# A graph layer with a feed-forward on one core: sums of gathered messages made, copied, turned and added in pairs

## What is computed

```python
hx = jnp.einsum('ni,rio->rno', layernorm(x), weight)           # 6250 nodes, 256 features, 8 relations
agg = jax.ops.segment_sum(hx[edge_type, src], dst, num_segments=6250)   # 206250 edges, sorted by dst
x1 = x + agg * 0.5 ** 0.5 + h_bias + (layernorm(x) @ loop_weight) * 0.5 ** 0.5
xn = layernorm(x1)
w = xn @ wr + br                                               # one weight a node
y = (gelu(xn @ w1 + b1) @ w2 + b2) * w                         # 256 -> 1024 -> 256
out = x1 + xn + where(node is among the 3124 largest w, y, 0)
```

## Time and profile before

| | us |
|---|---|
| median of 3 runs | 2587.57 (2576.79 to 2591.49) |
| profiled execution, its own time | 2560.34 |
| span of that execution | 2558.7 |
| PE busy | 1869.3 (73%) |
| PE weight loads | 1529.2 (60%) |
| POOL busy | 1548.9 (61%) |
| DVE busy | 776.9 (30%) |
| ACT busy | 697.8 (27%) |

### The profile page before, as it was taken

One profiled execution on the slowest core, in us unless ns is written; L12 is line 12 of the kernel. 1 busy time (PEld: TensorE's weight loads), 2 busy tenths in 40 slices (PEclk: granted clock), 3 DMA queues, 4 the chain that ended last, 5 costly groups with the idle time before them and its releaser, 6 DMA issues.

```text
span 2558.7 us, 25060 instructions
## 1 busy us (share of the span) xinstructions
PE 1869.3 (73%) x8680; PEld 1529.2 (60%) x8680; DVE 776.9 (30%) x1714; ACT 697.8 (27%) x1341; POOL 1548.9 (61%) x1737
## 2 busy tenths in 40 slices
PE   1237878777877877887877877877877877877881
PEld 0126657666665665665666666756656665666671
DVE  6112322232232232232232232232232232222337
ACT  5102223223222222222322322223223223223240
POOL 2666666666666666666666666666666666666500
PEclk9568888887887898887988988888988887887895
DMA  7533333333333333333333333333333333333315
GB/s 254 158 88 98 98 99 95 93 103 97 97 103 95 97 101 97 96 100 97 99 103 97 97 105 97 98 102 99 97 103 98 98 103 97 95 101 96 85 33 179
DMA packets 126598, 265.50 MB, mean 104 GB/s; under 512 B 30091, under 2 KB 73003, under 8 KB 126473
## 3 DMA queue, kind: packets, MB, share of 16 engines
q0 software_dynamic: 79168, 218.05, 29.6%
q1 hardware_dynamic: 47304, 45.83, 5.7%
HBM read 244.52 MB, written 19.25 MB: 103 GB/s over the span
## 4 chain that ended last, share of the span: by engine, by line
PE 55%; another core or an unknown queue 21%; issue 10%; ACT 8%; DVE 3%; DMA 1%; SPq 1%; DVEq 0%; POOL 0%; ACTq 0%; POOLq 0%
PE bank L642 21%; PE bank L670 13%; PE bank L688 7%; PE bank L696 7%; PE bank L652 4%; ACT hidden L541 2%; ACT stage L506 2%; PE bank L672 2%; ACT L541 1%; DMA acc<-in_edge_type 1%; DVE acc L1060 1%; ACT L528 1%; DMA w_sb<-in_L_ffn_w 1%; ACT normed_t L533 1%
## 5 line engine op out<-in xcount | busy, mean ns | idle before, releaser
L404 POOL DMA_INDIRECT messages<-normed_table,gather_rows x1614 | 1531.0, 949 | 854.3 <-issue 433.3
L642 PE MATMUL bank<-messages,onehot 128*128 128x256 f32 x3228 | 929.3, 423 | 124.9 <-issue 100.6
L642 PEld LDWEIGHTS bank<-messages,onehot 128*128 128x128 f32 x3228 | 642.6, 213 | 248.9 <-issue 179.0
L919 DVE SCALAR_TENSOR_TENSOR sums<-bank,regular,sums 128x256 f32 x538 | 259.9, 483 | 1657.4 <-remote 850.8
L506 ACT ACTIVATE stage<-bank 128x256 f32<-128x256 f32 x538 | 207.3, 388 | 1737.4 <-remote 1013.9
L652 PE MATMUL bank<-ident,stage 128*128 128x128 f32 x1076 | 234.4, 297 | 254.8 <-issue 158.8
L670 PE MATMUL bank<-rel_sb,closed 128*128 128x256 f32 x1568 | 361.6, 384 | 8.7 <-ACT closed L512 8.7
L652 PEld LDWEIGHTS bank<-ident,stage 128*128 128x128 f32 x1076 | 151.5, 152 | 336.1 <-issue 283.1
L688 PE MATMUL bank<-normed_t,w_sb 128*128 128x128 f32 x1568 | 240.0, 316 | 131.2 <-ACT normed_t L533 72.2
L670 PEld LDWEIGHTS bank<-rel_sb,closed 128*128 128x128 f32 x1568 | 302.3, 193 | 53.3 <-ACT closed L512 10.8
L688 PEld LDWEIGHTS bank<-normed_t,w_sb 128*128 128x128 f32 x1568 | 225.4, 229 | 147.1 <-ACT normed_t L533 85.6
(11 more groups left out here) (136 smaller groups left out, 519.8 us busy)
## 6 DMA issues: line engine op xcount, KB each, us to landing
messages<-normed_table,gather_rows POOLq DMA_INDIRECT x1614
normed_x<-normed_table SPq DMA_DIRECT2D x49, 128.0 KB
residual<-resid SPq DMA_DIRECT2D x49, 128.0 KB
x_block<-in_x SPq DMA_DIRECT2D x48, 128.0 KB
node_out<-acc SPq DMA_DIRECT2D x12, 512.0 KB
messages<-in_x POOLq DMA_DIRECT2D x6, 896.0 KB, 14.9
normed_table<-messages SPq DMA_DIRECT2D x6, 896.0 KB, 8.0
messages<-residual SPq DMA_DIRECT2D x6, 896.0 KB, 10.1
```

The lines of the kernel that those rows point to most:

```text
L404: pool.indirect_dma_start(messages[0:EP, g % RING, j * D:(j + 1) * D], None, table, bass.IndirectOffsetOnAxis(ap=gather_rows[0:EP, g, j:j ...
L642: last = nc.tensor.matmul(banks[g % STAGES][:, 0:D], onehot[0:EP, g % SLOTS, j, :], messages[0:EP, slot, j * D:(j + 1) * D], start=(j == 0 ...
L919: V.scalar_tensor_tensor(sums[:, :, to], banks[TURNS[g % 2]][:, 0:D].rearrange("p (n m) -> p n m", m=W), regular[:, 0:1], sums[:, :, to], ...
```

## The change

The tick stays, but sums, copies, turns and additions come at odd ticks, for two groups at once. The two groups of a pair share a bank of PSUM: the first in columns 0 to 255, the second in 256 to 511. One copy of 512 columns takes both to `stage`, four transposes turn them, and two additions add them. The turn is of the pair two before the one that is summed at that tick (LAG 4 in place of 2), and the closing tick of a block is made odd. `summed`, `staged` and `turned` count pairs; POOL waits once a pair, at its even group. The block's later steps move to later ticks: up from 9 to 10, gelu from 10 to 12, down from 12 to 14, `ffn_leave` from 13 to 16.

In the head, a partition holds seven neighbouring rows of the features (runs of 7 KB in memory in place of 1 KB). The sources are loaded first on SyncE's queue; destinations and types follow the features on POOL's. `index_stage` comes behind the last chunk in place of behind the third.

In the tail, the last block's up product is made in halves ahead of the first two counts, its down product in quarters ahead of the last four, and its `ffn_leave` comes behind the eighth round. The selection waits for the last w alone.

```diff
-    LAG = 2
+    LAG = 4
...
-    TURN, TURN_TAKE, UP, GELU, DOWN, LEAVE = 7, 8, 9, 10, 12, 13
+    TURN, TURN_TAKE, UP, GELU, DOWN, LEAVE = 7, 8, 10, 12, 14, 16
...
-    closing = {g + LAG: b for b, g in enumerate(closes)}
+    closing = {(g | 1) + LAG: b for b, g in enumerate(closes)}
...
-        table_chunks = table.rearrange("(c v p) d -> c p v d", p=P, v=CH)
+        table_chunks = table.rearrange("(c p v) d -> c p v d", p=P, v=CH)
...
-        stage = sb("stage", [P, STAGES, D])
+        stage = sb("stage", [P, STAGES, 2 * D])
...
-            sp.wait_ge(pads_set, 3)
-            for a, to in ((dst, dst_s), (src, src_s), (edge_type, type_s)):
-                sp.dma_start(to[:, 0:full_tiles, :], a[0:full_tiles * P * GE].rearrange("(t p e) -> p t e", p=P, e=GE)).then_inc(edges_in, 16)
-                sp.dma_start(to[0:rest, full_tiles, :], a[full_tiles * P * GE:NG_FULL * GE].rearrange("(p e) -> p e", e=GE)).then_inc(edges_in, 16)
-                sp.dma_start(to[rest:rest + 1, full_tiles, 0:E - NG_FULL * GE],
-                             a[NG_FULL * GE:E].rearrange("(p e) -> p e", p=1)).then_inc(edges_in, 16)
+            sp.wait_ge(pads_set, 1)
+            sp.dma_start(src_s[:, 0:full_tiles, :], src[0:full_tiles * P * GE].rearrange("(t p e) -> p t e", p=P, e=GE)).then_inc(src_in, 16)
+            sp.dma_start(src_s[0:rest, full_tiles, :], src[full_tiles * P * GE:NG_FULL * GE].rearrange("(p e) -> p e", e=GE)).then_inc(src_in, 16)
...
-            sp.wait_ge(summed, NG)
+            sp.wait_ge(summed, NG // 2)
...
+            pool.wait_ge(pads_set, 1)
...
+            x_chunks = x[0:last_first * P, :].rearrange("(c p v) d -> c p v d", p=P, v=CH)
...
+            nc.gpsimd.memset(dst_s[:, GT - 1, :], -1).then_inc(pads_set, 1)
+            nc.gpsimd.memset(type_s[:, GT - 1, :], 0).then_inc(pads_set, 1)
+            pool.wait_ge(pads_set, 3)
+            for a, to in ((dst, dst_s), (edge_type, type_s)):
+                pool.dma_start(to[:, 0:full_tiles, :], a[0:full_tiles * P * GE].rearrange("(t p e) -> p t e", p=P, e=GE)).then_inc(edges_in, 16)
+                pool.dma_start(to[0:rest, full_tiles, :], a[full_tiles * P * GE:NG_FULL * GE].rearrange("(p e) -> p e", e=GE)).then_inc(edges_in, 16)
+                pool.dma_start(to[rest:rest + 1, full_tiles, 0:E - NG_FULL * GE],
+                               a[NG_FULL * GE:E].rearrange("(p e) -> p e", p=1)).then_inc(edges_in, 16)
             nc.gpsimd.memset(ident[:, :], 0.0).then_inc(node_pad_set, 1)
...
-                if g >= RING:
-                    pool.wait_ge(summed, g - RING + 1)
+                if g >= RING and g % 2 == 0:
+                    pool.wait_ge(summed, (g - RING) // 2 + 1)
...
-            def stage_group(g):
-
-                act.wait_ge(summed, g + 1)
-                nc.scalar.activation(stage[:, g % STAGES, :], banks[g % STAGES][:, 0:D], ACT.Copy).then_inc(staged, 1)
+            def stage_pair(q):
+
+                act.wait_ge(summed, q + 1)
+                nc.scalar.activation(stage[:, q % STAGES, :], banks[q % STAGES][:, :], ACT.Copy).then_inc(staged, 1)
...
-                if g < NG:
-                    stage_group(g)
+                if g < NG and g % 2 == 1:
+                    stage_pair(g // 2)
...
-            def sum_group(g):
-
-                slot = g % RING
-                if g % 2 == 0:
-                    pe.wait_ge(onehot_ready, g // 2 + 1)
-                pe.wait_ge(gathered[slot], 16 * J * (g // RING + 1))
-                for j in range(J):
-                    last = nc.tensor.matmul(banks[g % STAGES][:, 0:D], onehot[0:EP, g % SLOTS, j, :],
-                                            messages[0:EP, slot, j * D:(j + 1) * D], start=(j == 0), stop=(j == J - 1))
+            def sum_pair(q):
+
+                pe.wait_ge(onehot_ready, q + 1)
+                for g in (2 * q, 2 * q + 1):
+                    slot = g % RING
+                    pe.wait_ge(gathered[slot], 16 * J * (g // RING + 1))
+                    for j in range(J):
+                        last = nc.tensor.matmul(banks[q % STAGES][:, g % 2 * D:(g % 2 + 1) * D], onehot[0:EP, g % SLOTS, j, :],
+                                                messages[0:EP, slot, j * D:(j + 1) * D], start=(j == 0), stop=(j == J - 1))
                 last.then_inc(summed, 1)
 
-            def turn_group(g):
-
-                if g >= 2:
-                    pe.wait_ge(sum_taken, g - 1)
-                pe.wait_ge(staged, g + 1)
-                for k in range(KC):
-                    last = nc.tensor.transpose(banks[TURNS[g % 2]][:, k * P:(k + 1) * P],
-                                               stage[:, g % STAGES, k * P:(k + 1) * P], ident[:, :])
+            def turn_pair(q):
+
+                if q >= 2:
+                    pe.wait_ge(sum_taken, 2 * q - 2)
+                pe.wait_ge(staged, q + 1)
+                for k in range(2 * KC):
+                    last = nc.tensor.transpose(banks[TURNS[q % 2]][:, k * P:(k + 1) * P],
+                                               stage[:, q % STAGES, k * P:(k + 1) * P], ident[:, :])
                 last.then_inc(turned, 1)
 
...
-            def ffn_first(b):
-                pe.wait_ge(ffn_norm_t, b + 2)
-                pe.wait_ge(ffn_done, 2 * b + 1)
-                for m in range(HC):
+            def ffn_first(b, first=0, past=HC):
+                if first == 0:
+                    pe.wait_ge(ffn_norm_t, b + 2)
+                    pe.wait_ge(ffn_done, 2 * b + 1)
+                for m in range(first, past):
                     for k in range(KC):
                         last = nc.tensor.matmul(banks[5 + m // 4][:, m % 4 * P:(m % 4 + 1) * P],
                                                 w1_sb[:, k, m * P:(m + 1) * P], normed_t[:, k, :],
                                                 start=(k == 0), stop=(k == KC - 1))
-                last.then_inc(ffn_up, 1)
-
-            def ffn_second(b):
-                pe.wait_ge(ffn_gelu, b + 2)
-                for m in range(HC):
+                if past == HC:
+                    last.then_inc(ffn_up, 1)
+
+            def ffn_second(b, first=0, past=HC):
+                if first == 0:
+                    pe.wait_ge(ffn_gelu, b + 2)
+                for m in range(first, past):
                     last = nc.tensor.matmul(banks[5][:, 0:D], hidden[:, m, :], w2_sb[:, m, :],
                                             start=(m == 0), stop=(m == HC - 1))
-                last.then_inc(ffn_down, 1)
+                if past == HC:
+                    last.then_inc(ffn_down, 1)
 
             pe.wait_ge(rel_in, 16 * KC)
             pe.wait_ge(ffn_w_in, 32)
             pe.wait_ge(loop_in, 16)
...
-                if LAG <= g < NG + LAG:
-                    turn_group(g - LAG)
-                if g < NG:
-                    sum_group(g)
+                if LAG <= g < NG + LAG and g % 2 == 1:
+                    turn_pair((g - LAG) // 2)
+                if g < NG and g % 2 == 1:
+                    sum_pair(g // 2)
...
-                if g - UP in closing:
+                if closing.get(g - UP, NB - 1) < NB - 1:
                     ffn_first(closing[g - UP])
-                if g - DOWN in closing:
+                if closing.get(g - DOWN, NB - 1) < NB - 1:
                     ffn_second(closing[g - DOWN])
 
             for r in range(8):
+                if r < 2:
+                    ffn_first(NB - 1, r * HC // 2, (r + 1) * HC // 2)
+                elif r >= 4:
+                    ffn_second(NB - 1, (r - 4) * HC // 4, (r - 3) * HC // 4)
                 pe.wait_ge(counts_in, r + 1)
                 nc.tensor.matmul(banks[0][:, 0:15], one_rows, pick_counts[:, :], start=True, stop=True).then_inc(counts_out, 1)
             pe.wait_ge(counts_in, 9)
...
-                if c == 2:
-                    index_stage()
+            index_stage()
...
-                dve.wait_ge(turned, g + 1)
+                if g % 2 == 0:
+                    dve.wait_ge(turned, g // 2 + 1)
                 to = bass.ds(places[g % LOAD], W)
                 if g:
                     dve.wait_ge(sum_taken, g)
-                if g - 1 in closed_at:
-                    dve.wait_ge(carried, closed_at[g - 1] + 1)
+                for before_it in (g - 1, g - 2):
+                    if g % 2 == 0 and before_it in closed_at:
+                        dve.wait_ge(carried, closed_at[before_it] + 1)
                 if g - 1 - WAIT_CLEAR in closed_at:
                     dve.wait_ge(slot_cleared, closed_at[g - 1 - WAIT_CLEAR] + 2)
-                V.scalar_tensor_tensor(sums[:, :, to], banks[TURNS[g % 2]][:, 0:D].rearrange("p (n m) -> p n m", m=W),
+                V.scalar_tensor_tensor(sums[:, :, to], banks[TURNS[g // 2 % 2]][:, g % 2 * D:(g % 2 + 1) * D].rearrange("p (n m) -> p n m", m=W),
                                        regular[:, 0:1], sums[:, :, to], ALU.mult, ALU.add).then_inc(sum_taken, 1)
 
             def carry(b):
...
```

(17 more changed lines are left out.)

27 lines of the change are left out of this document (15 added, 12 removed).

## The result

| | us |
|---|---|
| before, median of 4 runs | 2586.26 (2576.79 to 2591.49) |
| after, median of 4 runs | 2703.93 (2701.44 to 2705.57) |
| ratio after to before, 95% interval | 1.0458 (1.0427 to 1.0490) |
| profiled execution after: own time, span | 2701.44, 2699.7 |

What follows compares the result with a forecast made beforehand. The prediction took POOL's gathers and their ring waits for late-seen TensorE sums as the bound. From 2560.3, head -9, end -9.5, drain +1 and middle 0 gave 2542.8; with 27.2 for the median, 2570 us, range 2430 to 2655.

Steps and rivals of the forecast that it cites:

- Head, -9: Before the first gather: index work moved behind the last feature chunk lets gathers start earlier; -9 us, bounds 0 and -14.
- End, -9.5: After the last gather: selection no longer waits for the last feed-forward, whose halves and quarters are mostly hidden; -9.5 us.
- my mark of 1 us: Tail check in the changed profile: the selection should start within 1 us of the last weights.
- Drain, +1: Behind the last sum: 2 more transposes and a longer copy, about +1 us.
- Turns: TensorE's waits ahead of transposes, 158.8 + 80.8 us, would thin out; taken as worth nothing, middle being POOL's.
- Pairs at the relation products: Both products between two pair sums, 11.0 us against 7.5 of gathers; cost between 0 and 108 us, taken as 0.
- The bound of +108: Upper bound in the middle for longer ring gaps at the relation products: (5.3 - 3.1) x 49 = 108 us.
- The lateness: TensorE's finished work seen late (8.1 us) during gather runs, soon after POOL stops; copies should still start many microseconds late.
- The 27 us between profile and median: Median of before lies 27.2 us above its profiled execution; the same was expected of the changed kernel.
- the sum of 2542.8: Forecast of the changed kernel's profiled execution: 2560.3 - 9 - 9.5 + 1 + 0 us.
- The second: Rival: coarser ring release lengthens the gap at the relation products, 2624 to 2678 us; chance 0.27.
- The first: Rival: freed TensorE waits shorten the ring's gaps, 40 us or more in the middle; chance 0.20.

Runs made afterwards that it cites:

- paced_later_again: products_later with a 64-column memset on GpSimd and a wait for its end before each group of gathers; 2693.7 us against 2558.0 before, chip B.
- head_tail: Kernel before with the changed head and end only, single groups, old turn lag and ticks; 2560.5 us against 2587.6 before, chip A.
- products_later: Changed kernel with relation products and following steps two ticks later, two spare ticks before the last block; 2549.0 us on A, 2558.5 on B when repeated.
- close_ahead: Changed kernel with ScalarE's closed copy ahead of the closing tick's pair copy, two spare ticks before the last block; 2611.6 us against 2587.6 before, chip A.
- after_third: The changed kernel, unedited, on prompt-signal chip E; 2185.6 us against 2195.1 before, ratio 0.9958.
- release_by_group: Changed kernel with each group freeing its ring place at its own sum's end, copies, turns and adds still paired; 2674.1 us against 2587.6 before, chip A.
- one_behind_later: products_later with LAG = 2, the turn one pair behind the sum; 2173.5 us against 2195.3 before, chip C.
- both_ahead: close_ahead with ScalarE's copy of the turned loop input ahead of the pair copy too; 2174.2 us against 2195.1 before, chip D.

## Why the prediction was wrong

*Head, -9.* Right in kind, a low figure: -14.0 measured, the bound I had set. The trace of after puts the wait before the first gather down to ScalarE's copy of the keys, but the gathers ask only for the store of the features and for the tables of rows, which were taken long before the keys. In paced_later_again the same wait is put down to the store, as I had it:

```profile
55.02 0.16 POOL L415 MEMSET pace<- 128x64 f32 x1 [26.17 <-DMA normed_table<-closed]
```

*End, -9.5.* Right on its own: -12.3 in head_tail. In the changed kernel it is spoiled. The selection starts at 2639.39, 6.6 us behind the last weight (2632.58 + 0.21), and my mark of 1 us fails, because it stands behind `ffn_leave` of the last block but one:

```profile
2632.58 0.21 DVE L980 TENSOR_SCALAR w_all<-w_block,br_b 128x1 f32<-128x1 f32 x1
2633.26 5.29 PE L709 MATMUL bank<-w_sb,hidden 128*128 128x256 f32 x16 [4.43 <-ACT hidden L551]
2638.66 0.42 DVE L986 TENSOR_TENSOR acc<-bank,b_b 128x256 f32<-128x256 f32 x1 [5.86 <-PE bank L709]
2639.39 0.18 DVE L1030 TENSOR_SCALAR routing<-w_all 128x49 int32<-128x49 int32 x1
```

*Drain, +1.* Mis-sized: +22.6 against head_tail behind the last gather, of which 6.6 are this later start of the selection. From the last gather to the last weight after takes 84.1 us (2548.73 to 2632.79) and head_tail 67.6 (2431.64 to 2499.19). I had counted two transposes and a copy. But the drain begins with a wait of 9.16 us for `closed`, where head_tail's first one behind the last gather is 2.25 us, and its later hand-overs stand tighter too (4.17 us at the next `closed`, 4.43 at the down product):

```profile
2557.43 5.65 PE L680 MATMUL bank<-rel_sb,closed 128*128 128x256 f32 x16 [9.16 <-ACT closed L522]
```

*Turns.* Their waits fell from 240 to 78 us, and the kernel got no faster by it, as I had said. The reason is not the one I gave: the waits turned up elsewhere, as the next item says.

*Pairs at the relation products, "I take 0 here as well, since a longer gap also lets the late signals through".* This is the step that failed. It is the larger part of the 117 us that the pairs cost between the gathers, where I had put nothing. The rows of before gave the spacing of TensorE's work: 11.0 us of work against 7.5 us of ring. I asked how long the products keep the sums away, and never whether the products' own inputs would be there. TensorE's queue holds several instructions that need a late result: a turn needs the copy of a sum two back, the products need, by way of `closed`, the copy of the sum one back. In the kernel before, the turns came up first and took the waits: 240 us, and 8.7 us in 4 at the products. In the changed one a turn asks for what is two pairs old and passes, and TensorE runs on until the first instruction that asks for what is one pair old. The waits fell by 162 us at the turns (240 to 78) and rose by 151 at the products (8.7 to 159.4), but they didn't just change places: at the up product they rose as well, from 130.7 to 243.1, and I can't say how much of that comes of the same hand-overs. I had taken the first as a gain of nothing, and left out the others. What makes the same wait dearer there is only argued: behind a turn comes a sum, which frees the ring; behind the products' wait come 8 us of products, and in the block shown GpSimd used up its ring over them. That the place of the products and what they ask of ScalarE make most of the loss, three comparisons show: products_later gives back 155 us, and 123 on B, where only the tick of the products parts it from the slowest kernel; close_ahead, which but for its two spare ticks only gets `closed` ready earlier, gives back 92. The bound of +108 left out the same thing; it lies just under the 117.

*The lateness.* The mark held (7.2 us where 8.1 had been). But I wrote of it as something that comes with gathers. after_third has the same row of gathers without any, so gathers alone don't bring it; the sort of chip has a part, which the trace of one chip couldn't tell. I also wrote that finished work is seen soon after GpSimd has had to stop: 47 of the 120 late copies of after start with gathers going on.

*The 27 us between profile and median.* I carried them over to the changed kernel. Its profiled execution is 2701.4 with a median of 2703.9; head_tail's is 2561.7 with 2560.5. The offset belonged to one execution of the kernel before. By own times the sum of 2542.8 missed by 158.6: middle +144.7, of which 27.8 are this offset and 116.9 the pairs, end and drain +18.8, head -5.0. As a base for the median the 27 us were in place (2587.6 - 17.5 = 2570); as an offset between profile and median that every kernel has they were not.

*Rivals.* The second (coarser release, 2624 to 2678, chance 0.27) named the right place, the right sign and a size that was too small, for another reason than the right one: release_by_group shows that the coarser release itself is 30 us of it. The first, freed waits, didn't occur.

A page and this trace: ScalarE's table load ahead of `closed` takes 1.28 us, with 1.31 between its neighbours (1273.14 + 0.38 to 1274.83). The Trainium skill, page "ScalarE: Activation LUTs", section "What ACT_TABLE_LOAD costs", gives 1283 ns for the load, which agrees, and some 1.4 us of drain more, which this place doesn't show; 94 of the 97 loads of after have the same 1.31 us between their neighbours. By the page's sum, as an estimate, the products would have waited 1.4 us longer than they did.

On the lateness itself, "Perfetto Trace Analysis" of the Trainium skill, section "Summary: the profiler window per engine type", says that a TensorE row ends at an estimated time and leaves out the way of the signal. The 7.2 us may thus lie in matmuls that really end later or in the signal; no run here separates the two. One thing the trace does rule out: the record of the update of `summed` stands 0.02 us before the copy's start for 117 of the 120 late copies, and never at the sum's recorded end. So it isn't ScalarE that looks late; the update comes late.

## What to carry to other kernels

When results of one engine are seen late by another, lengthening the lag of one hand-over need not end the wait; here waits came up at the next instructions of the queue that ask for a recent result. List these in the queue's order with the age of what each needs, follow each through the other engine's queue to what stands ahead of it there, and give all of them the new lag at once: here two ticks more for the consumer gave 123 to 155 us, and the producer's place ahead of the pair copy that waits for the late signal 92. And before tuning against a wait of unclear origin, measure on another chip: on one sort this change is 4.6% slower, on the other 0.4% faster. Nor is there one best version: products_later is 1.4% faster than before on one slow-signal chip and equal on the other, head_tail 0.9% faster (one chip), one_behind_later and both_ahead 1.0% faster where signals are prompt.

## What the runs showed of the hardware

The kernel before took 2587.6 and 2558.0 us on chips A and B, and 2195.3, 2195.1 and 2195.1 on C, D and E, each within 1% from run to run. For the changed kernel, whose traces on both sorts are kept, the difference lies in waits: 992.4 us of idle time before gathers against 518.2, with gathers (947 and 950 ns) and copies (601 and 597) nearly the same. The mean granted clock is 0.838 in after and 0.953 in after_third; in after TensorE is also busy for less of the span, 70% against 79%. On the slow-signal chips TensorE also halts inside runs of matmuls: 166.1 us in the up product of after for no cause that the profile shows, where after_third has none. I don't know the cause of these halts, nor of the late updates of TensorE's semaphores (120 of 269 in after, none in after_third), while what ScalarE signals reaches TensorE in 0.05 us on both sorts of chip (25 waits for `closed` in after, one in after_third).
